# Attention over a long context: each cycle's work block moved behind its value products, and the accumulators' copy and one key centring moved on VectorE

## The chip, the cores and the metric

One Trainium2 chip, of which the program uses one core. The metric is the time of one execution on the device, in microseconds (us). The kernel before was run three times and takes 408.71 us (median; 408.44 to 408.76).

## What is computed

Cross attention for 16 batches with 16 heads of width 8: 100 queries and 1444 keys per batch, everything in fp32.

```python
Q = relu(x @ Wq + bq);  K = relu(ctx @ Wk + bk);  V = relu(ctx @ Wv + bv)
scores = einsum('hbqd,hbkd->hbqk', Qh, Kh) / sqrt(8)
attn = softmax(where(key_mask == 0, NEG, scores)) * q_mask
out = einsum('hbqk,hbkd->hbqd', attn, Vh) + x
```

The kernel leaves the maximum out of the softmax: it takes the exponential of centred scores, and a check at the end chooses a slower general path if a bound is passed. With these inputs the general path isn't taken.

## The kernel before

A batch's 1444 keys are padded to 12 tiles of 128, and each tile is handled in two halves of eight heads: 24 units per batch. For a unit, TensorE makes scores (`scores`, L508, 4 matmuls, 64-row tiles of the array) into one of three PSUM slots; ScalarE takes their exponential (L434, one instruction of 128x800) into one of six `probs` slots; TensorE multiplies them with the values (`value_products`, L523, 32-column tiles) and accumulates in the bank `o_ps` over the whole batch. Scores run `LEAD` = 3 units ahead.

TensorE's program is written out by hand. A batch has 8 cycles of three units. Each cycle is three blocks: **scores** of units u+3 to u+5, one block of **work**, **value products** of units u to u+2. The work uses one PSUM bank, `work_ps`, which VectorE must have emptied (`work_free`) before the next work block. Over the 8 cycles the work is: four value projections of the next batch (L466, 3 matmuls each), three key projections of the batch after next (L461; 512, 512 and 420 columns), and the transposes of the previous batch's outputs (L472). Batch 0 has an order of its own (`FIRST_SIDE_WORK`): its cycle 6 has two key projections, one ahead of the scores and one behind them, and its cycle 7 has the third. The last batch has only the transposes and two small checks. Batches 1 to 12 run in a hardware loop of two batches per turn (`pairs_loop`, L251); 0, 13, 14 and 15 are written out.

VectorE empties each work block: `finish_values` (L766, L767, then three L774), `read_keys` (L731), and after the third key chunk `split_keys`, which finds the maximum and writes `k_high` and `k_cent` (L745, 1444 columns each). `finish_keys` makes `k_low` (L750) from the two. `finish_outputs` (L805 to L819) normalises the transposed outputs. `copy_outputs` (L798) copies `o_ps` to `o_sb`; it signals `o_copied`, without which the next batch's first value product must not start, since it overwrites `o_ps`. SyncE sends `k_high` and `k_low` by 16 DMAs per batch to `k_parts`. VectorE executes in order; in batch 0 it also has two long sums over the queries (`max_queries` L892, `mask_queries` L885) between the last values and the first key chunk of batch 2.

In the views "PE" is TensorE, "PEld" its weight loads, "DVE" VectorE, "ACT" ScalarE.

Of the kernel before, what the change touches and what calls it, by code (L numbers as in the profile page):

```python
# [32 lines left out]
def attention(  # L33
# [12 lines left out]
    B, SQ, D = x.shape  # L46
# [43 lines left out]
    with ctx:  # L90
# [25 lines left out]
        k_cent = sb("k_cent", [P, SKP])  # L116
# [79 lines left out]
        work_filled = sem("work_filled")  # L196
# [4 lines left out]
        k_cent_ready = sem("k_cent_ready")  # L201
# [250 lines left out]
        def _(pe):  # L452
# [60 lines left out]
            def value_products(b, parity, u):  # L513

                kt, half = divmod(u, HALVES)
                if u == 0:
                    pe.wait_ge(v_ready, (KT + 1) * (b + 1))
                    if not isinstance(b, int) or b > 0:
                        pe.wait_ge(o_copied, b)
                pe.wait_ge(probs_ready, UNITS * b + u + 1)  # L520
                for c in range(HALF_PAIRS):
                    n, tile = divmod(c, TILES)
                    mm = nc.tensor.matmul(  # L523
                        o_ps[c * VCOLS:(c + 1) * VCOLS, half * PCOLS:(half + 1) * PCOLS],
                        values[:, parity, kt, half * HALF_PAIRS + c, :],
                        probs[:, u % PROB_SLOTS, tile, n * PCOLS:(n + 1) * PCOLS],

                        start=(u == 0), stop=(kt == KT - 1), skip_group_check=True)
                mm.then_inc(pv_done, 1)
# [14 lines left out]
            def batch(b, parity, first=False, last=False, keys=True):  # L544
                used = works_before(b)
                side = FIRST_SIDE_WORK if first else LAST_SIDE_WORK if last else SIDE_WORK

                def next_scores(u):
                    if u < UNITS:
                        scores(b, parity, u)  # L550
                    elif not last:
                        scores(b + 1, 1 - parity, u - UNITS)

                def side_work(step):
                    nonlocal used
                    k, ahead = step
                    if step == OUTPUTS:
                        work(used)
                        pe.wait_ge(o_copied, b)
                        transpose_outputs().then_inc(work_filled, 1)  # L560
                        used = used + 1
                    elif keys or ahead == NEXT:
                        prepare(b + ahead, (parity + ahead) % 2, k, used)
                        used = used + 1

                for cycle in range(CYCLES):
                    units = range(cycle * CYCLE, (cycle + 1) * CYCLE)
                    for step in side[cycle][:-1]:
                        side_work(step)
                    for u in units:  # L570
                        next_scores(u + LEAD)
                    for step in side[cycle][-1:]:
                        side_work(step)
                    if last and cycle == CYCLES // 2:
                        check_batches(used)
                    if last and cycle == CYCLES // 2 + 1:
                        count_batches()
                    for u in units:
                        value_products(b, parity, u)
                return used  # L580

            def check_batches(used):
# [135 lines left out]
        def _(dve):  # L718
# [24 lines left out]
            def center_keys(target, parity, done):  # L743

                v.tensor_scalar(target[:, 0:SK], k_raw[:, 0:SK], 0.0, k_max[:, parity:parity + 1], ALU.max, ALU.subtract  # L745
                                ).then_inc(done, 1)
# [48 lines left out]
            def copy_outputs(b):  # L795

                dve.wait_ge(pv_done, UNITS * (b + 1))
                v.tensor_copy(o_sb[:], o_ps[:, 0:HALVES * PCOLS]).then_inc(o_copied, 1)  # L798

            def finish_outputs(b, index):  # L800

                dve.wait_ge(work_filled, index + 1)
                t = work_ps[0:SQ, :].rearrange("q (rj c w) -> q rj c w", c=HALF_PAIRS, w=VCOLS)

                v.tensor_scalar(inv_den[:], t[:, :, :, PAIR * DH], DEN_FLOOR, None, ALU.max).then_inc(den_read, 1)  # L805
                dve.wait_ge(den_read, b + 1)
                v.reciprocal(inv_den[:], inv_den[:]).then_inc(den_inverted, 1)
                dve.wait_ge(den_inverted, b + 1)
                o = o_norm[:].rearrange("q (r c j d) -> q r c j d", r=HALVES, c=HALF_PAIRS, j=PAIR)
                t = work_ps[0:SQ, :].rearrange("q (r j c w) -> q r j c w", r=HALVES, j=PAIR, w=VCOLS)  # L810
                i = inv_den[:].rearrange("q (r j) c -> q r j c", j=PAIR)
                for j, done in ((0, o_half_normed), (1, work_free)):
                    v.tensor_tensor(o[:, :, :, j, :], t[:, :, j, :, j * DH:(j + 1) * DH],  # L813
                                    i[:, :, j, :].unsqueeze(3).to_broadcast([SQ, HALVES, HALF_PAIRS, DH]),
                                    ALU.mult).then_inc(done, 1)
                dve.wait_ge(o_half_normed, b + 1)
                dve.wait_ge(work_free, index + 1)
                at = slice(b, b + 1) if isinstance(b, int) else bass.ds(b, 1)
                v.scalar_tensor_tensor(out=x_rows(b), in0=o_norm[:], scalar=q_mask[:, at], in1=x_rows(b),  # L819
                                       op0=ALU.mult, op1=ALU.add).then_inc(out_ready, 1)  # L820

            def split_keys(b, parity, used):

                max_keys(b, parity, used)
                if isinstance(b, int) and b == 1:
                    dve.wait_ge(first_k_selected, KCHUNKS * QUADS)
                else:
                    dve.wait_ge(k_replicated, 16 * REPLICAS * (b - 1))
                center_keys(k_high, parity, k_high_ready)
                center_keys(k_cent, parity, k_cent_ready)  # L830

            def finish_keys(b):

                dve.wait_ge(k_high_ready, b + 1)
                dve.wait_ge(k_cent_ready, b + 1)
                low_keys(k_low_ready)

            def first_batch():
                for c in range(KCHUNKS):
                    read_keys(1, c, c)  # L840
                split_keys(1, 1, KCHUNKS)
                finish_keys(1)
                dve.wait_ge(values_zeroed, 2)
                used = KCHUNKS
                finish_values(1, 1, 0, used)
                dve.wait_ge(mask_step, 1 + QUAD)
                dve.wait_ge(q_replicated, 16 * REPLICAS)
                spread_queries(1, 1)
                for g in range(1, VGROUPS):
                    finish_values(1, 1, g, used + g)  # L850
                finish_keep(1, 1)
                max_queries()
                bound_scores(0, 0)
                bound_scores(1, 1)
                mask_queries()
                used = used + VGROUPS
                for c in range(KCHUNKS):
                    read_keys(2, c, used + c)
                split_keys(2, 0, used + KCHUNKS)

            def batch(b, parity, last=False, keys=True):
                used = works_before(b)
                copy_outputs(b - 1)
                if last:
                    finish_outputs(b - 1, used)
                    return used + 1
                finish_keys(b + 1)
                for g in range(VGROUPS):
                    finish_values(b + 1, 1 - parity, g, used + g)
                    if g == 0:  # L870
                        spread_queries(b + 1, 1 - parity)
                finish_keep(b + 1, 1 - parity)
                bound_scores(b + 1, 1 - parity)
                used = used + VGROUPS
                if keys:
                    for c in range(KCHUNKS):
                        read_keys(b + 2, c, used + c)
                    used = used + KCHUNKS
                    split_keys(b + 2, parity, used)
                finish_outputs(b - 1, used)  # L880

            def mask_queries():
# [54 lines left out]
            pairs_loop(dve, 1, B - 3, batch)  # L937
            batch(B - 3, (B - 3) % 2)
            batch(B - 2, (B - 2) % 2, keys=False)
            used = batch(B - 1, 1, last=True)  # L940


            dve.wait_ge(checks_summed, 1)
# [9 lines left out]
            dve.wait_ge(checks_summed, 2)  # L953
            v.tensor_copy(bounded[:], work_ps[0:1, 0:1]).then_inc(path_chosen, 1)
            copy_outputs(B - 1)
            finish_outputs(B - 1, used)

            def flat(ap, parts=P):
                return ap.rearrange("p (c n) -> p c n", n=BANK)
# [86 lines left out]
```

## Time and profile before

| | us |
|---|---|
| Median of three runs | 408.71 |
| The profiled execution | 409.39 |
| its span, first to last instruction | 407.6 |
| TensorE busy in the span | 389.7 (96%) |
| ScalarE busy | 305.4 (75%) |
| VectorE busy | 231.0 (57%) |
| GpSimd busy | 14.1 (3%) |
| Mean granted TensorE clock, of full | 0.986 |

The profiled execution is 0.68 us above the median, and 1.79 us of it lie outside the span. From about 79 us to 333 us each batch takes the same 23.06 us. Two places differ: a wait of TensorE near 50 us, in batch 0, and one near 335 us, where the loop ends; behind each, TensorE runs at half its clock for some microseconds.

### The profile page before, as it was taken

The page shows a single profiled execution, that of the slowest core. Times are in us where ns is not written, and L with a number is a line of the kernel's source. Part 1 is how long each engine was busy: PE and PEld are TensorE (multiplying, and loading weights), DVE is VectorE, ACT ScalarE, POOL GpSimd, SP SyncE. Part 2 cuts the span into 40 slices and gives each one's busy share as a digit, 9 for nine tenths or more (in the row PEclk, how much of TensorE's full clock was granted, in tenths as well). Part 3 has the DMA queues.
Part 4 walks back from the last instruction along what each step waited for, and adds up shares of the span by engine and source line. Part 5 has one row for each costly group of instructions (what it writes and reads, how often), then busy time and mean ns, then how long its engine had stood idle before and what let it go on. Part 6 is the DMA issues. An engine that isn't in the chain of part 4 may idle for free.

```text
span 407.6 us, 13727 instructions
## 1 busy us (share of the span) xinstructions
PE 389.7 (96%) x5216; PEld 265.1 (65%) x5216; DVE 231.0 (57%) x717; ACT 305.4 (75%) x408; POOL 14.1 (3%) x25
## 2 busy tenths in 40 slices
PE   7889699999999999999999999999999988999995
PEld 5756357675767667575767667575766656667663
DVE  1968756473838466473847557473847554366111
ACT  2687548787878787787878787787887864787993
POOL 9400000000000000000000000000000000000000
PEclk9999989999999999999999999999999996999999
DMA  7783616362634526172543616172543615025000
GB/s 238 193 288 154 224 55 238 104 253 87 242 126 163 205 91 238 57 278 73 227 141 149 219 73 242 53 290 78 212 156 136 232 54 226 21 93 209 7 7 8
DMA packets 20960, 62.52 MB, mean 153 GB/s; under 512 B 4938, under 2 KB 10954, under 8 KB 20938
## 3 DMA queue, kind: packets, MB, share of 16 engines
q1 hardware_dynamic: 20218, 61.32, 40.3%
q10 hardware_dynamic: 720, 0.89, 0.7%
q8 instruction: 17, 0.28, 0.3%
q14 instruction: 5, 0.04, 0.0%
HBM read 13.73 MB, written 0.82 MB: 36 GB/s over the span
## 4 chain that ended last, share of the span: by engine, by line
PE 87%; DVE 6%; issue 3%; POOL 2%; ACT 1%; DVEq 0%; ACTq 0%; POOLq 0%
PE psum L523 35%; PE psum L508 26%; PE psum L466 13%; PE psum L461 11%; PE psum L472 2%; POOL selectors L363 2%; DVE k_raw L731 1%; ACT probs L434 1%; DVE k_cent L745 1%; DVE v_biased L767 1%; DVE values L774 1%; DVE k_high L745 1%; DVE q_sum L885 1%; DVE k_parts L899 0%; POOL selectors L356 0%
## 5 line engine op out<-in xcount | busy, mean ns | idle before, releaser
L434 ACT ACTIVATE probs<-psum 128x800 f32<-128x800 f32 x384 | 293.2, 840 | 83.7 <-PE psum L508 83.7
L523 PE MATMUL psum<-probs,values 128*32 128x200 f32 x3072 | 158.5, 340 | 0.7 <-issue 0.7
L508 PEld LDWEIGHTS psum<-query_bd,k_parts 64*128 64x128 f32 x1536 | 97.5, 189 | 48.8 <-ACT probs L434 30.4
L523 PEld LDWEIGHTS psum<-probs,values 128*32 128x32 f32 x3072 | 87.6, 110 | 63.1 <-ACT probs L434 30.4
L508 PE MATMUL psum<-query_bd,k_parts 64*128 64x200 f32 x1536 | 121.5, 289 | 4.7 <-issue 3.0
L731 DVE TENSOR_SCALAR_CACHE_REDUCE k_raw<-psum,bk_sb 128x512 f32<-128x512 f32 (+1 forms) x48 | 34.4, 719 | 85.3 <-PE psum L461 85.2
L466 PE MATMUL psum<-wv_sb,keyT 128*128 128x129 f32 x384 | 59.8, 294 | 0.5 <-DVE v_biased L767 0.5
L461 PE MATMUL psum<-keyT,wk_mixed 128*128 128x512 f32 (+1 forms) x96 | 51.2, 618 | 3.8 <-DVE k_raw L731 3.8
L466 PEld LDWEIGHTS psum<-wv_sb,keyT 128*128 128x128 f32 x384 | 48.2, 193 | 7.3 <-DVE v_biased L767 0.8
L774 DVE TENSOR_SCALAR values<-v_biased,keep 128x128 f32<-128x128 f32 x192 | 43.4, 283 | 6.9
L767 DVE TENSOR_TENSOR v_biased<-psum,bv_sb 128x384 f32<-128x384 f32 x64 | 35.0, 547 | 0.0
L766 DVE TENSOR_SCALAR keep<-psum 128x3 f32<-128x3 f32 x64 | 10.1, 158 | 39.7 <-PE psum L466 39.7
L750 DVE TENSOR_TENSOR k_low<-k_cent,k_high 128x1444 fp32r<-128x1444 f32 (+2 forms) x18 | 26.6, 1487 | 0.2
L461 PEld LDWEIGHTS psum<-keyT,wk_mixed 128*128 128x128 f32 x96 | 14.7, 190 | 10.3 <-DVE k_raw L731 4.0
L789 DVE TENSOR_TENSOR query_bd<-query_rep,blockmask 128x200 fp32r<-128x200 f32 x60 | 17.9, 360 | 0.0
L745 DVE TENSOR_SCALAR k_high<-k_raw,k_max 128x1444 fp32r<-128x1444 f32 x16 | 16.0, 1001 | 1.7
L745 DVE TENSOR_SCALAR k_cent<-k_raw,k_max 128x1444 f32<-128x1444 f32 x16 | 16.6, 1037 | 0.0
L798 DVE COPY o_sb<-psum 128x400 f32<-128x400 f32 x16 | 9.1, 570 | 5.4 <-PE psum L523 4.4
L472 PE MATMUL psum<-ident,o_sb 128*100 128x128 f32 x64 | 10.3, 283 | 0.8 <-DVE o_sb L798 0.8
L805 DVE TENSOR_SCALAR inv_den<-psum 100x16 f32<-100x16 f32 x16 | 2.7, 169 | 11.7 <-PE psum L472 11.7
L819 DVE SCALAR_TENSOR_TENSOR x_sb<-o_norm,q_mask,x_sb 100x128 f32 (+1 forms) x16 | 5.6, 352 | 4.4 <-DVE o_norm L813 4.1
L425 ACT ACTIVATE k_parts<-psum 128x512 fp32r<-128x512 f32 (+1 forms) x12 | 5.8, 594 | 3.1 <-PE psum L612 3.1
(61 smaller groups left out, 96.6 us busy)
## 6 DMA issues: line engine op xcount, KB each, us to landing
k_parts<-k_high SPq DMA_DIRECT2D x120, 180.5 KB, 2.2
k_parts<-k_low SPq DMA_DIRECT2D x120, 180.5 KB, 2.2
keyT<-in_ctxT SPq DMA_DIRECT2D x15, 722.0 KB, 4.2
query_rep<-k_parts SPq DMA_DIRECT2D x16, 200.0 KB, 2.3
x_sb<-in_x SPq DMA_DIRECT2D x1, 800.0 KB
out<-x_sb SPq DMA_DIRECT2D x16, 50.0 KB
values<-in_xT ACTq DMA_DIRECT2D x1, 600.0 KB, 6.7
keyT<-in_ctxT SPq DMA_DIRECT2D x2, 256.0 KB, 4.0
```

What stands on the lines that cost most here:

```text
L434: nc.scalar.activation(probs[:, u % PROB_SLOTS], scores_ps[:, u % SCORE_SLOTS, :, 0:QCOLS], ACT.Exp, scale=SCALE).then_inc(probs_ready, 1)
L461: return nc.tensor.matmul(bank[:, 0:end - c * BANK], wk_mixed[:], keyT[:, parity, c * BANK:end], start=True, stop=True)
L466: return nc.tensor.matmul(bank[:, n * VW:(n + 1) * VW], keyT[:, parity, kt * P:(kt + 1) * P], wv_sb[:], start=True, stop=True)
L472: mm = nc.tensor.transpose(work_ps[0:SQ, n * P:(n + 1) * P], o_sb[:, n * SQ:(n + 1) * SQ], ident[:])
L508: mm = nc.tensor.matmul(scores_ps[:, u % SCORE_SLOTS, j, n * TCOLS:(n + 1) * TCOLS], k_parts[rows, parity, t, kt * P:(kt + 1) * P], query_ ...
L523: mm = nc.tensor.matmul(o_ps[c * VCOLS:(c + 1) * VCOLS, half * PCOLS:(half + 1) * PCOLS], values[:, parity, kt, half * HALF_PAIRS + c, :], ...
L731: v.tensor_scalar(k_raw[:, c * BANK:end], bank[:, 0:end - c * BANK], bk_sb[:], None, ALU.add, ALU.max, accum_out=k_chunk_max[:, c:c + 1]). ...
L745: v.tensor_scalar(target[:, 0:SK], k_raw[:, 0:SK], 0.0, k_max[:, parity:parity + 1], ALU.max, ALU.subtract).then_inc(done, 1)
L750: v.tensor_tensor(k_low[:, at], k_cent[:, at], k_high[:, at].bitcast(F32), ALU.subtract).then_inc(done, 1)
L767: v.tensor_tensor(v_biased[:, g % 2], work[:, :, 0:D], bv_sb[:].unsqueeze(1).to_broadcast([P, VGROUP, D]), ALU.add).then_inc(free, 1)
L774: v.tensor_scalar(values[:, parity, kt, :, 0:PAIR * DH], v_biased[:, g % 2, n].rearrange("p (a w) -> p a w", w=PAIR * DH), 0.0, keep[:, kt ...
L789: ins = v.tensor_tensor(query_bd[:, parity, t, :].rearrange("p (h q) -> p h q", h=TILE_HEADS), src[:, t].bitcast(F32).unsqueeze(1).to_broa ...
```

## The change

On TensorE, the three blocks of a cycle come in the order scores, value products, work. The work that stood ahead of the scores (the first of two in batch 0's cycles 0 and 6) stays there. In the last batch, the two checks come behind the value products.

On VectorE, `copy_outputs(b)` moves from the start of batch b+1 to the end of batch b, behind `k_high` and ahead of `finish_outputs(b - 1)`. It now first waits on `work_filled`, for the transposes, because these read the `o_sb` that it overwrites. `k_cent` moves from behind `k_high` to the start of the next batch; `finish_keys` (`k_low`) moves behind the first value group, and `spread_queries` behind the second. For batch 1's keys `k_cent` stays directly behind `k_high`. ScalarE's and SyncE's programs are the same.

```diff
                     for u in units:
                         next_scores(u + LEAD)
+                    for u in units:
+                        value_products(b, parity, u)
                     for step in side[cycle][-1:]:
                         side_work(step)
...
-                    for u in units:
-                        value_products(b, parity, u)
...
                 center_keys(k_high, parity, k_high_ready)
-                center_keys(k_cent, parity, k_cent_ready)
...
                 split_keys(1, 1, KCHUNKS)
+                center_keys(k_cent, 1, k_cent_ready)
                 finish_keys(1)
...
                 split_keys(2, 0, used + KCHUNKS)
-
-            def batch(b, parity, last=False, keys=True):
+                copy_outputs(0)
+
+            def batch(b, parity, keys=True):
                 used = works_before(b)
-                copy_outputs(b - 1)
-                if last:
-                    finish_outputs(b - 1, used)
-                    return used + 1
-                finish_keys(b + 1)
+                center_keys(k_cent, 1 - parity, k_cent_ready)
                 for g in range(VGROUPS):
                     finish_values(b + 1, 1 - parity, g, used + g)
                     if g == 0:
+                        finish_keys(b + 1)
+                    elif g == 1:
                         spread_queries(b + 1, 1 - parity)
...
+                dve.wait_ge(work_filled, used + 1)
+                copy_outputs(b)
                 finish_outputs(b - 1, used)
```

TensorE at the end of batch 0 and into batch 1 (L461 are the second and third key projections of batch 2; behind the branch L251 is batch 1), before:

```order
L461 MATMUL psum<-keyT,wk_mixed 128x512
L523 MATMUL psum<-probs,values 32x200 x12
L508 MATMUL psum<-query_bd,k_parts 128x200 x12
L461 MATMUL psum<-keyT,wk_mixed 128x420
L523 MATMUL psum<-probs,values 32x200 x12
L251 UNCONDITIONAL_BRANCH
```

and after:

```order
L523 MATMUL psum<-probs,values 32x200 x12
L461 MATMUL psum<-keyT,wk_mixed 128x512
L508 MATMUL psum<-query_bd,k_parts 128x200 x12
L523 MATMUL psum<-probs,values 32x200 x12
L461 MATMUL psum<-keyT,wk_mixed 128x420
L251 UNCONDITIONAL_BRANCH
```

The third key projection now stands next to batch 1's first scores, behind which batch 1's first value products follow at once.

VectorE at the end of a batch in the loop, before:

```order
L745 TENSOR_SCALAR k_high<-k_raw,k_max 128x1444 [waits k_replicated]
L745 TENSOR_SCALAR k_cent<-k_raw,k_max 128x1444
L802 REGISTER_ALU
L805 TENSOR_SCALAR inv_den<-psum 100x16 [waits work_filled]
L807 RECIPROCAL inv_den<-inv_den 100x16 [waits den_read]
```

and after:

```order
L745 TENSOR_SCALAR k_high<-k_raw,k_max 128x1444 [waits k_replicated]
L880 REGISTER_ALU
L797 REGISTER_ALU [waits work_filled]
L798 COPY o_sb<-psum 128x400 [waits pv_done]
L805 TENSOR_SCALAR inv_den<-psum 100x16 [waits work_filled]
L807 RECIPROCAL inv_den<-inv_den 100x16 [waits den_read]
```

The copy now stands between the transposes and the normalising, behind a register step that waits for the transposes; `k_cent` is no longer there.

## Rows read from the trace of the kernel before

**Rows 1.** The page: TensorE's busy line, and its granted clock in 40 slices.

```profile
PE 389.7 (96%) x5216; PEld 265.1 (65%) x5216; DVE 231.0 (57%) x717; ACT 305.4 (75%) x408; POOL 14.1 (3%) x25
...
PEclk9999989999999999999999999999999996999999
```

**Rows 2.** Timeline, one value cycle: start us, us, engine, line, operation, count [idle before].

```profile
201.96 0.92 PE L508 MATMUL psum<-query_bd,k_parts 64*128 64x200 f32 x12
...
202.48 2.29 ACT L434 ACTIVATE probs<-psum 128x800 f32<-128x800 f32 x3 [0.57 <-PE psum L508]
...
202.81 0.94 PE L466 MATMUL psum<-wv_sb,keyT 128*128 128x129 f32 x6
...
203.68 1.22 PE L523 MATMUL psum<-probs,values 128*32 128x200 f32 x24
...
204.83 0.92 PE L508 MATMUL psum<-query_bd,k_parts 64*128 64x200 f32 x12
```

**Rows 3.** Timeline of TensorE: work to value products, in the loop.

```profile
208.54 1.13 PE L461 MATMUL psum<-keyT,wk_mixed 128*128 128x512 f32 x2
...
209.60 1.22 PE L523 MATMUL psum<-probs,values 128*32 128x200 f32 x24
```

**Rows 4.** Timeline of TensorE in batch 0: value products, work, scores.

```profile
43.38 1.22 PE L523 MATMUL psum<-probs,values 128*32 128x200 f32 x24
44.53 1.13 PE L461 MATMUL psum<-keyT,wk_mixed 128*128 128x512 f32 x2
45.59 0.92 PE L508 MATMUL psum<-query_bd,k_parts 64*128 64x200 f32 x12
```

**Rows 5.** Timeline of TensorE late in batch 14: scores, value products.

```profile
375.32 0.92 PE L508 MATMUL psum<-query_bd,k_parts 64*128 64x200 f32 x12
...
376.16 1.22 PE L523 MATMUL psum<-probs,values 128*32 128x200 f32 x24
```

**Rows 6.** Timeline around a batch's end in the loop, TensorE and VectorE.

```profile
216.56 0.15 DVE L739 TENSOR_SCALAR k_max<-k_max 128x1 f32<-128x1 f32 x1
...
216.85 0.97 DVE L745 TENSOR_SCALAR k_high<-k_raw,k_max 128x1444 fp32r<-128x1444 f32 x1
...
217.56 0.64 PE L472 MATMUL psum<-ident,o_sb 128*100 128x128 f32 x4
...
218.14 1.22 PE L523 MATMUL psum<-probs,values 128*32 128x200 f32 x24
...
220.10 0.57 DVE L798 COPY o_sb<-psum 128x400 f32<-128x400 f32 x1
...
221.00 1.22 PE L523 MATMUL psum<-probs,values 128*32 128x200 f32 x24
```

**Rows 7.** Timeline late in batch 14: transposes, and VectorE, idle until then.

```profile
383.00 0.65 PE L472 MATMUL psum<-ident,o_sb 128*100 128x128 f32 x4
...
383.69 0.17 DVE L805 TENSOR_SCALAR inv_den<-psum 100x16 f32<-100x16 f32 x1 [7.74 <-PE psum L472]
```

**Rows 8.** Timeline from batch 0's last cycles into batch 1.

```profile
50.34 1.37 PE L461 MATMUL psum<-keyT,wk_mixed 128*128 128x512 f32 x2 [3.83 <-DVE k_raw L731]
...
54.96 0.97 PE L461 MATMUL psum<-keyT,wk_mixed 128*128 128x420 f32 x2
...
55.87 1.22 PE L523 MATMUL psum<-probs,values 128*32 128x200 f32 x24
...
57.94 0.97 DVE L745 TENSOR_SCALAR k_cent<-k_raw,k_max 128x1444 f32<-128x1444 f32 x1
...
58.82 0.57 DVE L798 COPY o_sb<-psum 128x400 f32<-128x400 f32 x1
...
59.49 1.22 PE L523 MATMUL psum<-probs,values 128*32 128x200 f32 x24 [0.69 <-issue]
```

**Rows 9.** Windows: length, busy and count of each engine, PEclk, DMA share, GB/s.

```profile
51.09:54.50 3.41, 3.41 (x31) 1.69 (x32) 0.76 (x2) 0.00 (x0) 0.00 (x0) 0.50 0.00 0
...
337.81:341.22 3.41, 3.18 (x23) 2.64 (x26) 0.38 (x2) 2.29 (x3) 0.00 (x0) 0.50 0.62 244
341.22:344.63 3.41, 3.41 (x37) 2.19 (x30) 2.03 (x8) 0.95 (x2) 0.00 (x0) 0.50 0.63 247
```

**Rows 10.** Timeline where the loop has ended: batch 13's first scores.

```profile
338.04 1.18 PE L508 MATMUL psum<-query_bd,k_parts 64*128 64x200 f32 x9 [2.98 <-issue]
```

More of the change, by code:

```diff
@@ L939, in _ @@
             batch(B - 2, (B - 2) % 2, keys=False)
-            used = batch(B - 1, 1, last=True)
+            used = works_before(B - 1)
+            finish_outputs(B - 2, used)
             dve.wait_ge(checks_summed, 1)
@@ L955, in _ @@
             copy_outputs(B - 1)
-            finish_outputs(B - 1, used)
+            finish_outputs(B - 1, used + 1)
             def flat(ap, parts=P):
```

## The prediction

> **What bounds the kernel.** I read the page first, then the timeline of one cycle, then that of a batch's end, and last the two places where the pattern breaks. TensorE is busy 96% of the span, at full clock nearly throughout [rows 1]. In a cycle its blocks follow one another without a wait: scores at 201.96, work at 202.81, value products at 203.68, scores again at 204.83; that is 0.85 + 0.87 + 1.15 = 2.87 us. ScalarE waits 0.57 us for scores in each such cycle [rows 2]. So TensorE's own stream is the bound, and a batch costs what its blocks cost, start to start. The change removes no instruction from TensorE. It can act in three ways: by what a change of block type costs, by new waits, and by what the waits do to the clock.
>
> **Block changes: nothing.** The old pairs are scores to work, work to value products, value products to scores; the new ones are scores to value products, value products to work, work to scores. Each new pair already occurs somewhere. Scores to value products: 375.32 to 376.16 is 0.84 [rows 5], as scores to work is 0.85 [rows 2]. Value products to work: 43.38 to 44.53 is 1.15, the same as to scores. Work to scores: 44.53 to 45.59 is 1.06 [rows 4], and the same key block to value products is 208.54 to 209.60, 1.06 [rows 3]. A block's length doesn't depend on its follower; the sum over a cycle stays at 2.87. Only for a value projection followed by scores is there no row; I bound it at 0.02 us to either side of the 0.87 and take 0, as for the key block. ScalarE gets its next scores after the same three blocks, so its waits stay.
>
> **The other work moved on VectorE: nothing.** The work blocks come one value-product block later relative to the scores, but their distance from each other is unchanged, and so is VectorE's time to empty the bank. k_low comes about 2 us later; its eight DMAs are needed only for the scores of a batch that begins some 20 us later, and k_high's DMAs stand ahead of them on SyncE's queue anyway. Output stores are waited for only at the end. `k_cent` and `k_low` behind the batch's end lie beside cycles of 2.87 us in which VectorE has some 1.2 us to spare (it is busy 231.0 of 407.6 us in all [rows 1]).
>
> **The copy in the loop: 14 short waits.** The copy used to start at 220.10 and the value products that need it at 221.00. Now these follow the scores at once. From the start of the transposes (217.56) TensorE reaches them after 0.58 (transposes, 217.56 to 218.14 [rows 6]) + 0.85 (scores) = 1.43 us. The copy must wait for the transposes. An idle VectorE starts 0.69 us after their start [rows 7]. One register step with the wait stands between: from k_max's end, 216.56 + 0.15 = 216.71, to k_high at 216.85 is 0.14, where a plain signal takes 0.04 (383.00 + 0.65 to 383.69 [rows 7]); so 0.10 more. Copy 0.57 [rows 6], and from its end to the value products 0.10 (58.82 + 0.57 to 59.49 [rows 8]). Sum 0.69 + 0.10 + 0.57 + 0.10 = 1.46 against 1.43: a wait of 0.03 us. k_high ends at 216.85 + 0.97 = 217.82, that is 0.26 after the transposes began, and so covers nothing and blocks nothing. Batches 2 to 15 have this wait: 14 x 0.03 = +0.4 us. Bounds: 0 if the signals overlap with the array's emptying, 0.15 each (2.1 us) if the register step or three semaphores cost more on TensorE. I take 0.03, since each of its parts is a measured row.
>
> **The copy at the end of batch 0: one long wait.** Here the copy stands behind the third key chunk of batch 2 on VectorE, in both kernels. Before: this projection starts at 54.96; without a wait batch 1's value products would come after 0.91 + 1.15 + 0.85 + 0.87 = 3.78 us (key, value products, scores, work), at 58.74. They come at 59.49, so they wait 0.75. After: only the key block and the scores lie between, 0.91 + 0.85 = 1.76 us. The copy can start where k_cent started, 57.94 - 54.96 = 2.98 after the projection, and with 0.57 + 0.10 the value products start at 3.65 [rows 8]. They wait 1.89 us, and nothing can pass them on TensorE: the work and the next scores are behind, and ScalarE runs dry. The difference is **+1.14 us**. That k_cent has left VectorE's chain saves 0.88 of what it would otherwise be; the two blocks that no longer cover the copy (value products and work, 2.02 us) cost more. The longer wait ahead of it, 3.83 us for VectorE's sums over the queries, stays: between the last value projection and the second key projection of cycle 6 lie the same three blocks in both orders (value products, key, scores), and VectorE's chain starts at the former.
>
> **Sum.** +1.14 + 0.42 = +1.56 us. On the profiled execution: span 407.6 to 409.2, its time 409.39 to 410.95. On the median 408.71: **410.3 us**.
>
> **Rivals.**
>
> *Clock luck at the loop's end (faster or same).* TensorE stood still for 2.98 us where the loop ends [rows 10] and then had half the clock (1.2 GHz) in two stretches of 3.41 us, 337.81 to 344.63 [rows 9]. Near 51 us, after a still longer wait, only one stretch was slow. The work at half clock costs half of each stretch, 1.7 us. The new order puts value products in front of the work there, as after 51 us, and shifts the wait by 1.6 us. If one of the stretches goes, the sum is 1.56 - 1.7: 408.6. If both go: 406.9. Nothing in the rows says which; before, the pattern repeats well enough for runs within 0.3 us.
>
> *A second slow stretch at the start (slower still).* After the 3.83 us wait the new order runs the key block and scores first and then has the 1.89 us wait a little later. If this prolongs the low clock: +1.7, 412.0. By the Trainium skill (TensorE: Matmul & The Clock Gate, "Why this matters for your kernels") idle gaps between bursts of matmuls bring the clock down; the trace agrees for 3.83 and 2.98 us and has stayed up over the 0.75 us here, but has no row for a gap in between.
>
> *Longer waits at every batch's end (slower).* 0.15 instead of 0.03 us, by the bound above: 1.14 + 2.1, 412.0. For it: the value products wait for three semaphores. Against: so they do in the 59.49 row, from which I took the 0.10.
>
> *The start's wait isn't new (no change).* If the value products of cycle 6, now issued ahead of the second key projection, fill part of the 3.83 us without the rest moving back, 1.15 us return: 409.1. Against: the last value projection moves back by the same block.
>
> *Cheaper block changes (faster).* If each value projection to scores gave 0.02 us and each other new pair 0.01, a cycle would gain some 0.03, and 120 cycles 3.6 us: 406.7. Rows 3 to 5 speak against it: the pairs agree within 0.01.
>
> **How the numbers follow.** My forecast, 409.6 to 411.2, has a chance of 0.40. One slow stretch less, 408.6: 0.11; both less, 406.9: 0.07. A slow stretch more, 412.0: 0.15. Longer waits, 412.0: 0.10. The start without a new wait, 409.1: 0.12. Cheaper changes, 406.7: 0.05. The range from 407.8 to 412.4 leaves out 0.12 below and some 0.08 above. A measurement of this kernel can tell about 0.2% (0.8 us) from no change. Faster by more: 0.07 + 0.05 = 0.12, and 0.13 with the tail of the 408.6 case. Same: 0.10 + 0.12 and the forecast's near edge, 0.25. Slower: 0.62.
>
> **What would show it.** Right: the period of a batch in the loop stays at 23.06 to 23.12 us; the copy starts about 0.8 us after the transposes; the first value products of batch 1 have about 1.9 us of idle time before them; key, value and score blocks keep 1.06, 0.87 and 0.85. Wrong: a period shorter than 23.0 us or above 23.2; low-clock stretches of another number than one and two; the 3.83 us wait much changed.

## The result and the profile after

The changed kernel takes 410.28 us (median of 5 runs, 409.54 to 410.92), the kernel before 408.71 us beside it (5 runs, 408.16 to 408.80). The ratio is 1.0042, with a 95% interval from 1.0026 to 1.0057: slower by 1.6 us, outside noise. Forecast was 410.3 us.

The total agrees better than its parts, and that is in part luck. The profiled execution of the changed kernel is the quickest of its five, 409.54 us with a span of 407.7, only 0.1 above the span before. So I cut both spans, and that of a second profile of the same changed kernel (run e0, below; its profiled execution took 411.05 us), at the same four points of the work: the first block of scores in TensorE's program of batch 2, that of batch 13, that of batch 14, and the end.

| Stage, us | before | changed | changed, again |
|---|---|---|---|
| start, to batch 2's first scores | 80.89 | 81.95 | 83.54 |
| 11 batches in the loop | 253.70 | 253.97 | 253.98 |
| batch 13's first scores to batch 14's (the loop's end) | 29.26 | 27.01 | 26.64 |
| the rest | 43.75 | 44.77 | 45.14 |
| span | 407.6 | 407.7 | 409.3 |

The timeline of TensorE at the three cuts, before, columns as in [rows 2]:

```profile
80.89 0.92 PE L508 MATMUL psum<-query_bd,k_parts 64*128 64x200 f32 x12
...
334.59 0.47 PE L508 MATMUL psum<-query_bd,k_parts 64*128 64x200 f32 x3
...
363.85 0.92 PE L508 MATMUL psum<-query_bd,k_parts 64*128 64x200 f32 x12
```

and in the changed kernel:

```profile
81.95 0.92 PE L508 MATMUL psum<-query_bd,k_parts 64*128 64x200 f32 x12
...
335.92 0.47 PE L508 MATMUL psum<-query_bd,k_parts 64*128 64x200 f32 x3
...
362.93 0.74 PEld L508 LDWEIGHTS psum<-query_bd,k_parts 64*128 64x128 f32 x12 [0.18 <-issue]
```

**Start.** The timeline from batch 0's last cycles into batch 1, to be held against [rows 8]:

```profile
45.41 1.10 PE L461 MATMUL psum<-keyT,wk_mixed 128*128 128x512 f32 x2 [0.81 <-DVE v_biased L767]
...
51.49 1.20 PE L461 MATMUL psum<-keyT,wk_mixed 128*128 128x512 f32 x2 [2.98 <-DVE k_raw L731]
...
56.09 0.97 PE L461 MATMUL psum<-keyT,wk_mixed 128*128 128x420 f32 x2
...
57.00 0.92 PE L508 MATMUL psum<-query_bd,k_parts 64*128 64x200 f32 x12
...
59.07 0.57 DVE L798 COPY o_sb<-psum 128x400 f32<-128x400 f32 x1
...
59.74 1.22 PE L523 MATMUL psum<-probs,values 128*32 128x200 f32 x24 [1.83 <-issue]
```

The third key projection begins at 56.09, the copy 2.98 us behind it, batch 1's value products 3.65 us behind it: both to the digit as summed. Their wait is 1.83 us where it was 0.69; the difference is the +1.14 of the forecast. The stage as a whole is 1.06 us longer. The long wait ahead of it, 3.83 us in [rows 8], is split: 0.81 us at batch 2's first key projection and 2.98 at the second, 3.79 together.

**A batch's end in the loop**, against [rows 6]:

```profile
219.90 0.64 PE L472 MATMUL psum<-ident,o_sb 128*100 128x128 f32 x4
...
220.47 0.92 PE L508 MATMUL psum<-query_bd,k_parts 64*128 64x200 f32 x12
220.68 0.57 DVE L798 COPY o_sb<-psum 128x400 f32<-128x400 f32 x1 [0.52 <-PE psum L472]
...
221.35 1.22 PE L523 MATMUL psum<-probs,values 128*32 128x200 f32 x24
```

The copy starts 0.78 us after the transposes (0.79 summed), the value products 1.45 us after them (1.46 summed; 1.43 without the wait). The batch takes 253.97 / 11 = 23.09 us, before 23.06: 0.03 per batch, as forecast. The pair of blocks for which the forecast had no row, a value projection followed by scores, takes 0.86 or 0.87 us, start to start, so nothing comes from there.

**The rest: a wait that the forecast lacks.** VectorE and TensorE at the end of batch 13:

```profile
363.04 0.57 DVE L798 COPY o_sb<-psum 128x400 f32<-128x400 f32 x1 [0.52 <-PE psum L472]
...
363.53 0.17 DVE L805 TENSOR_SCALAR inv_den<-psum 100x16 f32<-100x16 f32 x1
...
365.27 0.25 DVE L807 RECIPROCAL inv_den<-inv_den 100x16 f32<-100x16 f32 x1 [1.58 <-issue]
...
365.96 0.94 PE L466 MATMUL psum<-wv_sb,keyT 128*128 128x129 f32 x6 [0.96 <-DVE o_norm L813]
```

In the middle of `finish_outputs` VectorE stands still for 1.58 us without waiting for anyone ("issue"). The normalising ends later, the work bank comes free later, and batch 14's first value projection waits 0.96 us. That is the +1.02 of the last stage.

**The loop's end: a gain that the forecast has only in part, and as a rival.** TensorE's own stop where the loop ends, against [rows 9, 10]; the windows' columns are those of [rows 9]:

```profile
338.48 0.70 PE L508 MATMUL psum<-query_bd,k_parts 64*128 64x200 f32 x9 [2.09 <-issue]
```

```profile
335.72:339.13 3.41, 1.32 (x18) 0.86 (x17) 2.50 (x7) 0.80 (x2) 0.00 (x0) 1.00 0.43 167
339.13:342.54 3.41, 3.41 (x32) 2.24 (x30) 0.00 (x0) 2.01 (x3) 0.00 (x0) 0.50 0.48 186
342.54:345.95 3.41, 3.41 (x50) 2.58 (x51) 3.00 (x8) 2.30 (x3) 0.00 (x0) 1.00 0.22 90
```

The stop is 0.89 us shorter than in [rows 10], and only one stretch of 3.41 us at half clock follows, not two. The stage is 2.25 us shorter; what the stop doesn't explain, some 1.4 us, goes to the missing stretch. All the traces of this case, those of the experiments below too, show at this place:

| TensorE's order | stop, us | stretches at half clock behind it |
|---|---|---|
| old: before, e2, e7, e7b, e9 | 2.98, 2.21, 2.76, 2.21, 2.32 | 2, 1, 2, 1, 0 |
| new: changed, e0, e1, e3, e4, e5, e6, e8 | 2.09, 1.76, 2.19, 1.91, 1.95, 1.82, 1.82, 2.09 | 1, 1, 0, 1, 0, 1, 1, 1 |

So a shorter stop goes with TensorE's new order, 1.95 us against 2.50 on average; it is no accident of one execution. Two stretches followed only the two longest stops. The number of stretches otherwise varies within one order.

### The profile page after: what moved, and what is told of

Its sections match the earlier page's. It is cut to its first block, busy times and chain, and to the rows that moved or that the text cites. A ratio compares the mean times of both kernels' runs of the same rounds, so it can differ in the third digit from the quotient of the medians.

```text
span 407.7 us, 13741 instructions
## 1 busy us (share of the span) xinstructions
PE 387.8 (95%) x5216; PEld 265.2 (65%) x5216; DVE 232.6 (57%) x717; ACT 305.4 (75%) x408; POOL 14.1 (3%) x25
## 4 chain that ended last, share of the span: by engine, by line
PE 86%; DVE 7%; issue 3%; POOL 2%; ACT 1%; DVEq 0%; ACTq 0%; POOLq 0%
PE psum L523 35%; PE psum L508 26%; PE psum L466 13%; PE psum L461 11%; PE psum L472 2%; POOL selectors L363 2%; DVE k_raw L731 1%; ACT probs L434 1%; DVE k_cent L745 1%; DVE v_biased L767 1%; DVE values L774 1%; DVE k_high L745 1%; DVE q_sum L887 1%; DVE k_parts L901 0%; POOL selectors L356 0%
## 5 line engine op out<-in xcount | busy, mean ns | idle before, releaser
L523 PEld LDWEIGHTS psum<-probs,values 128*32 128x32 f32 x3072 | 88.9, 110 | 35.2 <-issue 2.1
L461 PE MATMUL psum<-keyT,wk_mixed 128*128 128x512 f32 (+1 forms) x96 | 51.0, 616 | 3.8 <-DVE k_raw L731 3.0
L461 PEld LDWEIGHTS psum<-keyT,wk_mixed 128*128 128x128 f32 x96 | 14.5, 188 | 19.2 <-issue 15.4
L472 PEld LDWEIGHTS psum<-ident,o_sb 128*100 128x100 f32 x64 | 6.3, 128 | 5.9 <-issue 5.9
```

What stands on the lines that cost most here:

```text
L461: return nc.tensor.matmul(bank[:, 0:end - c * BANK], wk_mixed[:], keyT[:, parity, c * BANK:end], start=True, stop=True)
L472: mm = nc.tensor.transpose(work_ps[0:SQ, n * P:(n + 1) * P], o_sb[:, n * SQ:(n + 1) * SQ], ident[:])
L523: mm = nc.tensor.matmul(o_ps[c * VCOLS:(c + 1) * VCOLS, half * PCOLS:(half + 1) * PCOLS], values[:, parity, kt, half * HALF_PAIRS + c, :], ...
```

## The experiments

Each kernel is compared with the kernel before, run beside it on the same chip: 408.44 us for e1 to e4, 408.98 for e0 and e5 to e7, 408.03 for e7b to e9. The medians of the kernel before differ by up to 0.95 us between these sets, so between sets the ratios say more than the times.

### e1: the start's wait, taken away

```diff
                 for c in range(KCHUNKS):
+                    if c == KCHUNKS - 1:
+                        copy_outputs(0)
                     read_keys(2, c, used + c)
                 split_keys(2, 0, used + KCHUNKS)
-                copy_outputs(0)
```

> The changed kernel, but in batch 0 VectorE copies the accumulators before it reads the third key chunk of batch 2, not behind k_high. Theory A (the 1.9 us wait of batch 1's first value products is what the change costs at the start): that wait goes, the time falls by 1.9 us, 410.3 to 408.4 us; the value products of batch 1 follow their scores after 0.2 us of emptying. Rival B (the 1.6 us come from the places with a low clock and from VectorE's 1.6 us gap in batch 13, the start's wait is given back later): within 0.4 us of the changed kernel, 410.3 us.

Measured: 407.61 us, ratio 0.9975 (0.9948 to 1.0002), where the changed kernel has 1.0042. The difference of the ratios is 2.7 us with some 1.3 us of uncertainty; 1.9 was expected. The timeline settles it:

```profile
56.11 0.97 PE L461 MATMUL psum<-keyT,wk_mixed 128*128 128x420 f32 x2
56.25 0.58 DVE L798 COPY o_sb<-psum 128x400 f32<-128x400 f32 x1 [2.50 <-PE psum L523]
...
57.01 0.92 PE L508 MATMUL psum<-query_bd,k_parts 64*128 64x200 f32 x12
...
57.86 1.22 PE L523 MATMUL psum<-probs,values 128*32 128x200 f32 x24
```

The third key projection begins at 56.11 as before (56.09), but the value products now follow at 57.86 and not at 59.74: 1.88 us. The copy lies beside the key projection, and nothing gives the gain back: batch 2's first block of scores begins at 80.07 us, where the changed kernel has 81.95, the same 1.88. Theory A holds. The profiled execution has no stretch at half clock at the loop's end; that part of its time is luck.

### e2, e3: each engine's part alone

e2 is the changed kernel with TensorE's old order:

```diff
                     for u in units:
                         next_scores(u + LEAD)
-                    for u in units:
-                        value_products(b, parity, u)
                     for step in side[cycle][-1:]:
                         side_work(step)
...
+                    for u in units:
+                        value_products(b, parity, u)
```

> Only VectorE's part of the change; TensorE keeps the old order (scores, work, value products). From the start of the transposes the last value products end at 0.57 + 1.15 + 0.1 = 1.8 us; the copy can start only then, and the normalising, which frees the work bank, behind it: copy 1.84, L805 2.32, bank free 3.2 us. The first value projection would come at 2.57 us, so it waits 0.64 us, 13 times: +8.3 us. At batch 0's end the wait of 0.75 us goes, since k_cent has left the chain. Theory A: 408.7 + 8.3 - 0.75 = 416.3 us. Rival B (a wait of this size hides, as TensorE's queue has other work): 408 to 409 us.

Measured: 420.02 us, ratio 1.028 (1.0236 to 1.0324). In the loop:

```profile
197.09 0.64 PE L472 MATMUL psum<-ident,o_sb 128*100 128x128 f32 x4
...
198.95 0.57 DVE L798 COPY o_sb<-psum 128x400 f32<-128x400 f32 x1 [1.60 <-PE psum L523]
...
200.34 0.94 PE L466 MATMUL psum<-wv_sb,keyT 128*128 128x129 f32 x6 [0.61 <-DVE o_norm L813]
```

The copy comes 1.86 and the projection 3.25 us after the transposes (1.84 and 3.2 expected), so a batch costs 0.68 us more (23.74). That is theory A, and rival B is out. But the time is 3.7 us above the expectation, and the excess is not in the loop. At the end of batch 13 the stop in `finish_outputs` is there again, longer and behind a later copy:

```profile
371.65 0.25 DVE L807 RECIPROCAL inv_den<-inv_den 100x16 f32<-100x16 f32 x1 [2.46 <-issue]
...
372.35 1.66 PE L466 MATMUL psum<-wv_sb,keyT 128*128 128x129 f32 x6 [3.11 <-DVE o_norm L813]
```

TensorE waits 3.11 us and then has half its clock for two stretches (371.63 to 378.45).

e3 is the kernel before with TensorE's new order, the same lines the other way round.

> Only TensorE's part of the change; VectorE keeps the old order, with the copy behind the normalising, and k_cent behind k_high. The copy starts 2.53 to 2.70 us after the transposes, and the value products could start at 3.3 us where they are due at 1.43: a wait of 1.86 us, 13 times, and 1.15 us in the last batch, 25.3 us; at batch 0's end the wait is 58.82 - 54.96 + 0.67 - 1.76 = 2.8 us where it was 0.75, +2.0. Theory A: 408.7 + 27.3 = 436 us. Rival B (the order of the blocks alone, which frees probs slots earlier, brings something that the waits hide): clearly below 434 us.

Measured: 446.61 us, ratio 1.0885 (1.0805 to 1.0965). The waits are as expected:

```profile
216.10 0.64 PE L472 MATMUL psum<-ident,o_sb 128*100 128x128 f32 x4
...
218.80 0.58 DVE L798 COPY o_sb<-psum 128x400 f32<-128x400 f32 x1 [0.20 <-issue]
...
219.48 1.45 PE L523 MATMUL psum<-probs,values 128*32 128x200 f32 x24 [1.88 <-issue]
```

The value products start 3.38 us after the transposes (3.3 expected) behind a wait of 1.88. The time is 10 us above the expectation, and that is the clock: a mean of 0.952 where it was 0.986. By the profile's page TensorE is idle 22 us longer than before, less than the 27 summed, and busy 14 us longer with the same instructions. Of the eleven loop waits of this kind (1.71 to 1.92 us, batches 2 to 12) six are followed by half clock and five are not; so is the wait of 2.71 us at batch 0's end. So such a wait can bring the clock down or not; in the changed kernel, which has one at the start, it did not in the first profile. That this order frees `probs` slots earlier brings nothing that shows beside these losses. The two parts cost 12 and 38 us alone and 1.6 together: only with VectorE's order does TensorE's cost next to nothing.

### e4: the key centrings together again

```diff
                 center_keys(k_high, parity, k_high_ready)
+                center_keys(k_cent, parity, k_cent_ready)
...
-                center_keys(k_cent, 1 - parity, k_cent_ready)
```

> The changed kernel with the two key centrings together again: k_cent directly behind k_high, ahead of the copy. Theory A: in the loop VectorE is free for the copy 1.06 us after the transposes' start, not 0.78; value products at 1.73 where 1.46, +0.27 us for 13 batches, 3.5 us, and the start's wait grows by 0.88: 410.3 + 4.4 = 414.7 us. Rival B (VectorE's chain behind k_high isn't what the value products wait for): 410.3 us.

Measured: 414.54 us, ratio 1.0147 (1.0102 to 1.0192).

```profile
201.98 0.64 PE L472 MATMUL psum<-ident,o_sb 128*100 128x128 f32 x4
202.15 0.97 DVE L745 TENSOR_SCALAR k_cent<-k_raw,k_max 128x1444 f32<-128x1444 f32 x1
...
203.03 0.57 DVE L798 COPY o_sb<-psum 128x400 f32<-128x400 f32 x1
...
203.70 1.22 PE L523 MATMUL psum<-probs,values 128*32 128x200 f32 x24 [0.23 <-issue]
```

Copy at 1.05, value products at 1.72 us after the transposes: 1.06 and 1.73 were summed. VectorE's chain behind k_high is what they wait for, to 0.01 us. That the time fits too, 414.5 for 414.7, is partly luck with the clock again: in this profile two more stretches at half clock follow the start's wait, now 2.71 us, and none the loop's end.

This run also shows VectorE's stop of batch 13, with `k_cent` back in its old place behind k_high:

```profile
367.47 0.97 DVE L745 TENSOR_SCALAR k_cent<-k_raw,k_max 128x1444 f32<-128x1444 f32 x1
...
370.55 0.25 DVE L807 RECIPROCAL inv_den<-inv_den 100x16 f32<-100x16 f32 x1 [1.55 <-issue]
...
371.24 0.94 PE L466 MATMUL psum<-wv_sb,keyT 128*128 128x129 f32 x6 [1.00 <-DVE o_norm L813]
```

### e0, e5: VectorE's stop in batch 13

e0 is the changed kernel once more; e5 adds to it, with `pad` a new tile:

```diff
                 bound_scores(b + 1, 1 - parity)
+                if isinstance(b, int) and keys:
+                    for n in range(9):
+                        v.memset(pad[:, n:n + 1], 0.0)
```

> The changed kernel as it is, once more, as the control for the three beside it on the same chip. Every theory: 410.3 us, between 409.5 and 411.0, with one to three stretches at the low clock between 40 and 370 us.

> The changed kernel with nine small memsets of an unused tile on VectorE in batch 13, where it is idle, behind the bounds' product. They shift VectorE's later code by nine instructions. Theory A (VectorE's 1.58 us gap between L805 and L807 in batch 13 is a fetch of its instructions at a fixed place in the code, which the removed k_cent used to cover): the gap moves nine instructions ahead, into the wait for the third key chunk, the first value projection of batch 14 waits no longer, and the time falls by 1.04 us, to 409.2 us. Rival B (the gap belongs to the reciprocal or to the semaphores there): it stays at L807 and so does the time.

Measured: e0 410.17 us, ratio 1.0042 (1.0023 to 1.0062); e5 409.51 us, ratio 1.0026 (1.0005 to 1.0046). The difference of 0.7 us, where 1.04 was expected, is within the noise of the two. The traces decide. In e5 (line numbers are higher by one):

```profile
361.12 0.57 DVE L799 COPY o_sb<-psum 128x400 f32<-128x400 f32 x1 [0.53 <-PE psum L473]
...
361.61 0.16 DVE L806 TENSOR_SCALAR inv_den<-psum 100x16 f32<-100x16 f32 x1
361.81 0.25 DVE L808 RECIPROCAL inv_den<-inv_den 100x16 f32<-100x16 f32 x1
...
363.01 0.94 PE L467 MATMUL psum<-wv_sb,keyT 128*128 128x129 f32 x6
```

The same instructions, in the same places of the same work, run through; the value projection follows its value products after 1.15 us without a wait. The stop goes with nine instructions ahead of it: it sits at a place in the code, not in the reciprocal. That it is a fetch of instructions is supported by the DMA view: between 363.4 and 364.1 us of the changed kernel, about where the stop begins, the queue q14, which carries only instructions, moves one packet:

```profile
q14 instruction: 1, 0.01, 4.1%
```

In the six traces with the stop (changed, e0, e1, e2, e4, e6) the reciprocal starts 1.7 to 2.0 us behind such a packet. In e5 the packet comes at 353.7 us, earlier in VectorE's program, between two key chunks; there VectorE is idle from 353.5 to 355.6 anyway.

In the kernel before, a packet comes between 362.2 and 363.0, and the stop doesn't show:

```profile
362.20 0.97 DVE L745 TENSOR_SCALAR k_cent<-k_raw,k_max 128x1444 f32<-128x1444 f32 x1
...
363.28 0.25 DVE L807 RECIPROCAL inv_den<-inv_den 100x16 f32<-100x16 f32 x1
```

`k_cent` runs beside the packet, but it is not what covers the stop, as the expectation of e5 had it: in e4 `k_cent` is back in that place, and the stop is there with 1.55 us. And here the reciprocal starts about 1 us behind the packet, sooner than in any trace with the stop, so it can hardly be what the packet brings. More likely the changed program of VectorE, with its added steps and its other order, puts this place of the code onto the reciprocal, where batch 14's first value projection depends on what follows. Which of its edits does that was not separated.

e0's second profile also shows how the total varies: its start is 1.6 us longer than the first profile's (83.54 against 81.95), and it has one more stretch at half clock there, behind the 1.83 us wait:

```profile
59.99:63.41 3.42, 3.42 (x32) 2.36 (x24) 0.55 (x1) 0.00 (x0) 0.00 (x0) 0.50 0.55 216
```

### e6, e7: without the long wait ahead

Both orders with VectorE's long sums out of batch 0's chain (the core of the edit; the product with `q_max` moves to batch 14):

```diff
-                max_queries()
-                bound_scores(0, 0)
-                bound_scores(1, 1)
-                mask_queries()
...
                     read_keys(2, c, used + c)
+                    if c == 0:
+                        bound_scores(0, 0)
+                        bound_scores(1, 1)
+                    if c < KCHUNKS - 1:
+                        mask_queries(c)
...
                 bound_scores(b + 1, 1 - parity)
+                if not keys:
+                    max_queries()
```

> The changed kernel with VectorE's two long sums over the queries (L894 and L887 of it, 4.1 us) taken out of batch 0's chain: the query mask's sum in two halves between the key chunks of batch 2, the queries' maximum in batch 14, multiplied with the key maxima in one instruction at the end; all is computed. Theory A (the wait of 3.0 us ahead of the second key projection is VectorE's sums, and the low clock behind it comes from the wait): 3.05 us and 1.6 us of slow clock go, 410.3 to 405.6 us. The 0.8 us wait of batch 2's first key projection for the last values, which the changed order has and the old one doesn't, stays. Rival B (a DMA or ScalarE ends the wait next): 409 us or more.

> The kernel before with the same two sums moved in the same way. Theory A: 3.83 us of wait and 1.6 us of slow clock go, 408.7 to 403.3 us; then the changed order is 2.3 us behind the old one (1.6 us of the change and the 0.8 us wait that the sums had hidden). Rival B (the two orders differ only by luck with the clock after the long wait): with the wait gone both give the same time within 0.5 us.

Measured: e6 404.94 us, ratio 0.9931 (0.9906 to 0.9956); e7 401.71 us, ratio 0.9832 (0.9806 to 0.9857). In both the wait and the slow stretch behind it are gone. The orders are now 3.2 us apart, with some 1.4 us of uncertainty; 2.3 was expected and at most 0.5 by rival B, which is out. e7 came out 1.6 us below its expectation; no run explains this. TensorE in e6:

```profile
43.67 0.94 PE L466 MATMUL psum<-wv_sb,keyT 128*128 128x129 f32 x6
45.42 1.10 PE L461 MATMUL psum<-keyT,wk_mixed 128*128 128x512 f32 x2 [0.81 <-DVE v_biased L766]
...
48.44 1.12 PE L461 MATMUL psum<-keyT,wk_mixed 128*128 128x512 f32 x2
...
52.40 0.92 PE L508 MATMUL psum<-query_bd,k_parts 64*128 64x200 f32 x12
55.24 1.22 PE L523 MATMUL psum<-probs,values 128*32 128x200 f32 x24 [1.92 <-issue]
```

Batch 2's first key projection waits 0.81 us: in batch 0's cycles 5 and 6 two work blocks now stand next to each other, and VectorE hasn't emptied the bank. The changed kernel has this wait too; there the longer one behind it is shorter by as much (2.98 for 3.83 us).

### e7b, e8, e9: do the sizes add

e8 is the changed order with all three mends (e1, e5, e6). e9 is e7 with the copy ahead of k_cent at batch 0's end:

```diff
                 center_keys(k_high, parity, k_high_ready)
+                if isinstance(b, int) and b == 2:
+                    copy_outputs(0)
                 center_keys(k_cent, parity, k_cent_ready)
```

> The kernel before with the two sums moved, once more, as the control for the two beside it: 401.7 us by every theory, between 400.5 and 404, as the low clock falls.

> The changed order with three mends together: the sums moved, batch 0's accumulators copied ahead of the third key chunk, and nine small memsets in batch 13 that shift VectorE's code. Theory A (the change costs just these places, and their sizes add): 404.9 - 2.0 (the wait of batch 1's first value products, 1.99 us in the trace with the sums moved) - 1.04 (batch 14's first value projection) = 401.9 us, level with the old order with its sums moved, 401.7. Rival B (the new order is slower by itself in the loop): 403 us or more.

> The old order with the sums moved, and at batch 0's end the accumulators' copy ahead of k_cent; in the loop the order of VectorE's work stays. Theory A: the 0.85 us that batch 1's first value products wait there go, 401.7 to 400.9 us, and this is the fastest. Rival B (VectorE's k_low, now behind the copy and k_cent as before, holds the first value projection's bank and takes the gain back): 401.7 us.

Measured: e7b 402.10 us, ratio 0.9855 (0.9837 to 0.9872); e8 401.86 us, 0.9850 (0.9826 to 0.9874); e9 402.80 us, 0.9876 (0.9849 to 0.9904). e8 comes out where the sizes put it, 401.9: mended in three places, the new order is level with the old one, and both are 1.5% faster than the kernel before. Each time is a median that contains the clock's stretches, so this confirms the sum to about 1 us, not each term. e9 is no gain; rival B is right:

```profile
54.31 1.67 DVE L750 TENSOR_TENSOR k_low<-k_cent,k_high 128x1444 fp32r<-128x1444 f32 x1
...
55.89 0.15 DVE L765 TENSOR_SCALAR keep<-psum 128x3 f32<-128x3 f32 x1
...
56.57 0.94 PE L466 MATMUL psum<-wv_sb,keyT 128*128 128x129 f32 x6 [1.03 <-DVE v_biased L766]
```

The value products no longer wait, but k_low still stands ahead of the first value group, and the next value projection waits 1.03 us for the bank. The changed kernel moved k_low behind that group; this shows why.

## Why the prediction was right, and where it was not

- *Block changes: nothing.* Right. The loop's batch is longer by the boundary's wait alone, 23.09 against 23.06 us, inside the 23.06 to 23.12 that was given as the sign.
- *The copy in the loop, 14 x 0.03.* Right, in each part (0.78 and 1.45 us measured).
- *The copy at batch 0's end, +1.14.* Right: 1.83 against 0.69 us of wait, and e1 removes 1.88 us.
- *The other work moved on VectorE: nothing.* This step failed in two places. It counted instructions, but took it for granted that VectorE's own code is always at hand: with the changed order a stop of some 1.6 us falls into `finish_outputs` of batch 13, 0.96 us of it reach TensorE, and that is the +1.02 us of the last stage. And "their distance from each other is unchanged" is wrong for batch 0's cycles 5 and 6, where value products had stood between two work blocks. The new wait there is 0.81 us; in the changed kernel it only takes its part of the 3.83 us (0.81 + 2.98), so it costs nothing, and it shows as a loss in e6.
- *Clock luck.* The first profile has one stretch less at the loop's end, as the first rival says, and the second profile has that and one stretch more at the start, as the second rival says. That the stop at the loop's end is itself shorter was in neither. Two of the signs that the forecast gave for being wrong thus came true: one and one stretch at half clock instead of one and two, and 2.98 us where the 3.83 us wait stood. The first came from the loop's end, the second from the 0.81 us above.

So for the median, the parts are 1.06 (start) + 0.3 (loop) + 1.0 (batch 13's stop), 2.4 us in all, and by difference from 1.57 some -0.8 from everything else: the shorter stop at the loop's end, and the number of half-clock stretches there and at the start. This remainder is inferred, not measured. Only two of the changed kernel's runs have a trace, with -2.25 and -2.62 at the loop's end and +1.06 and +2.65 at the start, and the kernel before has one. The forecast's 1.56 met the median because the missed stop and the remainder nearly cancel; that is luck. Its mechanism for the start and for the loop is right on its own.

What stays open: why the stop at the loop's end is shorter with the new order, which edit puts VectorE's stop onto the reciprocal, and what decides how many stretches at half clock follow a wait.

## What to carry to other kernels

When all block pairs cost the same, an order of blocks on the bounding engine is worth only what it does to the waits; so look for each wait whose cover it takes away, first of all at the places where the pattern is broken (the first batch, the loop's end, the last batches). When an engine's program is reordered, look in the trace for idle time of that engine with no releaser in the straight code behind the change; a few idle instructions ahead of it tell whether it sits at a place in the code. A total that agrees is no proof of its parts: cut both traces at the same points of the work and compare stage by stage.

## What the runs showed of the hardware

- VectorE can stop without a wait on anyone at a fixed place in straight code: 1.55 to 1.60 us in four traces (changed, e1, e4, e6), 1.90 in e0 and 2.46 in e2, at the same instruction; nine instructions ahead of it moved it away (e5). One packet on an instruction queue goes with it.
- TensorE stops where the hardware loop ends and straight code follows, in all thirteen traces: 2.21 to 2.98 us with the old order of blocks, 1.76 to 2.19 with the new one.
- Waits of 1.7 to 1.9 us on TensorE brought its granted clock to half (1.2 GHz) behind six of eleven in e3 and behind the start's wait of e0 (1.83 us), and not behind the start's waits of the first profile (1.83), e5 (1.82) and e6 (1.92).
- A VectorE copy behind a register step that carries the wait starts 0.14 us after the transposes' end (219.90 + 0.64 to 220.68), where a plain wait takes 0.04 ([rows 7]). From the end of the copy to the first matmul that waits for it are 0.10 us (59.07 + 0.57 to 59.74).
